# The text-and-image attention kernel: the first batch's value table copied inside the chip memory, the second batch's stored piece by piece

## The reference, cut to what matters

```python
q   = heads(x @ W_q)                                # x: 4 x 2048 x 640, 20 heads of 32
k_t, v_t = heads(text @ W_k), heads(text @ W_v)     # 73 text tokens per batch
probs_t  = softmax(q k_t^T * scale)
text_out = probs_t @ v_t
k_ip, v_ip = heads(ip @ W_k_ip), heads(ip @ W_v_ip) # 4 image tokens per batch
qsem  = l2norm(probs_t @ text);  ip_n = l2norm(ip)
fused = q k_ip^T * scale + 0.5 * (qsem . ip_n)
probs_ip = softmax(fused) * spatial_mask
out = (text_out + probs_ip @ v_ip) @ W_out + b_out + x
```

## Time and profile before

| | |
|---|---|
| three runs | 1017.63, 1020.25, 1022.09 us; median 1020.25 |
| the profiled execution | 1022.47 us, span 1020.6 us |
| TensorE clock granted, mean | 0.988 |
| prologue ends and main loop begins | 88.7 us into the span |
| step 16, the first with output products all through | 184.8 us |

### The profile page before, as it was taken

The page is one execution under the profiler, slowest core; times in us unless marked ns, Lnnn a source line. Parts: engine busy times, 40 slices in busy tenths (PEclk is TensorE's granted clock), DMA queues, the critical chain, the costliest instruction groups (busy, mean ns, idle before and its releaser), DMA issues.

```text
span 1020.6 us, 24929 instructions
## 1 busy us (share of the span) xinstructions
PE 969.2 (95%) x7684; PEld 803.6 (79%) x7684; DVE 816.6 (80%) x2409; ACT 695.6 (68%) x2332; POOL 655.2 (64%) x1906
## 2 busy tenths in 40 slices
PE   5987788999999999999999999999999999999988
PEld 5875666888878888888887888888878888888855
DVE  6685698888888887888888888878878888878872
ACT  3534887777776777767776777777667777777740
POOL 3224587776676667677766777676667767776761
PEclk9978999999999999999999999999999999999999
DMA  9936999989889998899899989998899989887973
GB/s 293 298 117 161 195 179 186 177 163 180 168 186 186 186 185 177 163 176 162 174 178 192 192 164 191 169 167 173 167 190 187 180 169 190 137 157 154 149 138 111
DMA packets 488147, 180.27 MB, mean 177 GB/s; under 512 B 449694, under 2 KB 467155, under 8 KB 488015
## 3 DMA queue, kind: packets, MB, share of 16 engines
q1 hardware_dynamic: 487983, 178.63, 86.3%
q10 hardware_dynamic: 32, 0.07, 0.0%
HBM read 42.34 MB, written 27.22 MB: 68 GB/s over the span
## 4 chain that ended last, share of the span: by engine, by line
PE 77%; DMA 5%; DVE 4%; ACT 2%; issue 2%; SPq 2%; POOL 1%; DVEq 0%; ACTq 0%; POOLq 0%
PE ps_O L1257 25%; PE ps_Q L1368 25%; PE ps_S L1278 12%; PE ps_U L1354 11%; DMA pts<-ph 4%; PE ps_M L1294 3%; ACT pr L1038 2%; DMA x_in<-in_x_dram 1%; SPq L951 1%; DVE pr L1199 0%; PE ps_U L1257 0%; DVE n L1211 0%; ACT ph L1050 0%; DVE bias L1160 0%; SPq L924 0%
## 5 line engine op out<-in xcount | busy, mean ns | idle before, releaser
L1038 ACT ACTIVATE pr<-ps_S,bias 128x73 f32<-128x73 f32 x1280 | 288.8, 339 | 101.3 <-DVE bias L1160 100.1
L1120 POOL TENSOR_TENSOR ph<-pr,ph 128x220 f16<-128x220 f32 (+1 forms) x640 | 274.0, 460 | 126.2 <-ACT ph L1050 126.2
L1368 PE MATMUL ps_Q<-xT,wq_hi 128*128 128x512 f32 x800 | 280.1, 415 | 5.2 <-DVE qT L1127 5.2
L1257 PE MATMUL ps_O<-wo_hi,aT 128*128 128x320 f16 x1220 | 279.2, 300 | 0.0
L1050 ACT ACTIVATE ph<-pr 128x292 f16<-128x292 f32 x640 | 241.2, 500 | 0.0
L1257 PE MATMUL ps_O<-wo_lo,aT 128*128 128x320 f16 x610 | 182.3, 299 | 0.0
L1354 PE MATMUL ps_U<-xm,pts 128*128 128x110 f16 (+1 forms) x2560 | 159.3, 212 | 14.9 <-DMA pts<-ph 13.5
L1368 PEld LDWEIGHTS ps_Q<-xT,wq_hi 128*128 128x128 f32 x800 | 146.2, 191 | 32.7 <-DVE qT L1127 6.5
L1354 PEld LDWEIGHTS ps_U<-xm,pts 128*128 128x128 f16 (+1 forms) x2560 | 144.4, 98 | 32.3 <-issue 11.8
L1278 PE MATMUL ps_S<-kbd,qT 128*128 128x308 f32 x960 | 163.0, 304 | 2.6 <-ACT pr L1038 2.1
L1278 PEld LDWEIGHTS ps_S<-kbd,qT 128*128 128x128 f32 x960 | 150.8, 188 | 18.6 <-issue 3.0
(11 more groups left out here) (228 smaller groups left out, 1338.9 us busy)
## 6 DMA issues: line engine op xcount, KB each, us to landing
out_dram<-x_in SPq DMA_DIRECT2D x64, 320.0 KB, 2.6
x_in<-in_x_dram SPq DMA_DIRECT2D x56, 320.0 KB, 3.2
pts<-ph SPq DMA_TRANSPOSE x320, 3.4
w_k<-in_L_xattn_W_k_dram SPq DMA_DIRECT2D x5, 512.0 KB, 8.8
w_ip<-in_L_xattn_W_k_ip_dram SPq DMA_DIRECT2D x1, 2560.0 KB, 11.0
w_v<-in_L_xattn_W_v_dram SPq DMA_DIRECT2D x5, 512.0 KB, 8.3
w_ip<-in_L_xattn_W_v_ip_dram SPq DMA_DIRECT2D x1, 2560.0 KB, 10.6
x_in<-in_x_dram SPq DMA_DIRECT2D x2, 1280.0 KB, 7.2
```

The costliest lines, as they stand in the source:

```text
L1038: last = nc.scalar.activation(pr[p % P_RING][:, j, h, :], sc[:, j, h, 0:T], ACT.Exp, bias=bias[p % 2][:, j, h:h + 1], scale=SCALE)
L1120: nc.gpsimd.tensor_tensor(lo, full[:, :, t0:t1], one[:, :, 0, t0:t1], ALU.subtract).then_inc(pl_ready, 1)
L1257: last = nc.tensor.matmul(bank[:, 0:HALF], stationary, moving, start=(k, a, b_) == O_MMS[0], stop=(k, a, b_) == O_MMS[-1])
L1368: last = nc.tensor.matmul(ps_Q[:], wq[a][:, c, k * P:(k + 1) * P], xT[(CC * i + c) % XT_RING][b_][:], start=(c, a, b_) == Q_MMS[0], stop=( ...
```

## The change

Batch 0's eight pieces go from `xb[0]` directly to their rows of `xm`; each counts on `xm_loaded[0]`. Its ten reads from `x_d` are gone, and the wait for the stores ahead of them. Batch 1's eight pieces are stored to `x_d` one a step in steps 2 to 9, at the head of SP's step. The two batches' halves of the buffer are moved so that batch 0's lies within `x_in[2]` and batch 1's within `x_in[3]`. SP awaits the direct copies before the first load of x tile 2 (step 1), and batch 1's stores before the first load of x tile 3 (step 11). PE awaits all eight copies before the first value product.

```diff
-        xb = [one[0:T, 0:4 * HEADS * XW].rearrange("t (b k h w) -> t b k h w", b=2, k=2, w=XW)
-              for one in (late0[:].bitcast(F16), late1)]
+        xb = [one[0:T].rearrange("t (b n) -> t b n", b=2)[:, :, 0:2 * HEADS * XW]
+              .rearrange("t b (k h w) -> t b k h w", k=2, w=XW) for one in (late0[:].bitcast(F16),)]
+        xb.append(late1[0:T, 0:4 * HEADS * XW].rearrange("t (b k h w) -> t b k h w", b=2, k=2, w=XW))
...
                 if p == FIRST:
                     for tile, row, part, t0, t1 in pieces:
-                        sp.dma_start(x_d[0:2, tile, row:row + t1 - t0].rearrange("b t h w -> t b h w"),
-                                     xb[0][t0:t1, :, part]).then_inc(x_d_stored, 16)
+                        sp.dma_start(xm[row:row + t1 - t0, tile], xb[0][t0:t1, 0, part]).then_inc(xm_loaded[0], 16)
+                if 0 <= p - 2 < len(pieces):
+                    tile, row, part, t0, t1 = pieces[p - 2]
+                    sp.dma_start(x_d[1, tile, row:row + t1 - t0], xb[0][t0:t1, 1, part]).then_inc(x_d_stored, 16)
...
-                        if p == max(2 * SLOTS * b + 2 * c - 6, FIRST):
-
-                            if b:
-                                sp.wait_ge(u_ready, 2 * (SLOTS * b + c) - 8)
-                            if c == 0 and b < 2:
-                                sp.wait_ge(x_d_stored, 16 * 8)
+                        if b and p == 2 * SLOTS * b + 2 * c - 6:
+
+                            sp.wait_ge(u_ready, 2 * (SLOTS * b + c) - 8)
                             for tile, n in enumerate(STACK):
                                 sp.dma_start(xm[0:n, tile, c * HG:(c + 1) * HG, :],
                                              x_d[b, tile, 0:n, c * HG:(c + 1) * HG, :]).then_inc(xm_loaded[c], 16)
...
                         if p == max(STEPS * j + LOAD_AT[q], FIRST):
+                            if j == 2 and q == 0:
+                                sp.wait_ge(xm_loaded[0], 16 * len(pieces))
+                            if j == 3 and q == 0:
+                                sp.wait_ge(x_d_stored, 16 * len(pieces))
...
-                        pe.wait_ge(xm_loaded[k0], 32 * (slot // SLOTS + 1))
+
+                        b = slot // SLOTS
+                        if b:
+                            pe.wait_ge(xm_loaded[k0], 32 * b + (0 if k0 else 16 * 8))
+                        elif k0 == 0:
+                            pe.wait_ge(xm_loaded[0], 16 * 8)
```

## The result

The changed kernel took 1024.03 us (median of seven runs, 1020.75 to 1026.07) against 1020.25 us before (seven runs, 1017.63 to 1022.52). The two medians differ by 3.8 us. The ratio estimated from all fourteen runs is 1.0031, 95% interval 1.0018 to 1.0045: slower by 0.31%, about 3.2 us, less than the 0.5% set as the bound.

A forecast was written before the change was run, and what follows sets the result against it. It took DVE and the DMA engines, with SP third, as near full in steps 2 to 9. Terms -0.1 + 0.2 + 0.3 + 0.5 + 0.9 + 0.4 = +2.2 us on 1020.25 gave 1022.4 us, range 1017.2 to 1026.6 us.

The forecast's parts named there:

- What bounds the kernel: Steps 2 to 9: DVE and DMA engines near full, SP third; PE full from step 16, so delay passes one to one.
- Part 1: Loop start: eight direct copies replace eight stores and eight reads; nothing on the path, -0.1 us.
- the sign that I had set against it: At the loop start: pair 0's transposes issued before 104.3 us would prove the start's forecast wrong.
- The cover: At the start: copies done by 93.0 to 101.0 us, far ahead of the first value product at 108.55 us.
- the bounds of the copies' own price: At the start, from 88.7 us: direct copies done between 93.0 us (4.3 us) and 101.0 us (12.3 us).
- Part 2: SP in steps 2 to 9: eight issues added, two reads removed; lateness 0 to 0.5 us a step, -0.2 in step 2.
- Part 3: DMA engines in steps 2 to 9: 941 KB added, 188.2 KB removed, 3.5 to 4.9 us more of all sixteen engines.
- What reaches the path: Steps 2 to 9: +0.2, +0.3, +0.5 in steps 2 to 4, 0 in 5 to 7, +0.9 in 8, +0.4 in 9.
- hidden: Rival, steps 2 to 9: DVE's work and SP's gaps absorb everything; total -0.3 to +0.8 us; chance 0.20.
- The start was the limit: Rival, steps 0 to 2: without reads and with SP free they come earlier, -0.5 to -3 us; chance 0.12.
- The full engines pass it all on: Rival, steps 2 to 9: each store delays every later transpose on full DMA engines, +3.5 to +6.5 us; chance 0.18.
- The Trainium skill's price: Steps 2 to 9: bytes over 436 GB/s, 2.2 us added and 0.4 us removed; total about +1 instead of +2.2 us.

The follow-up runs named there:

- e1: Changed kernel with batch 1's eight stores all at the main loop's start, behind the direct copies, none in steps 2 to 9; ratio 0.9997 to the kernel before.
- e2: Changed kernel with batch 0 again going through chip memory and its reads back, batch 1's stores still spread; ratio 1.0028 to the kernel before.
- e6: e1 plus eight tiny stores (64 bytes of each row) in steps 2 to 9; ratio 1.0010 to the kernel before.
- e4: The changed kernel unaltered, timed again and profiled a second time; ratio 1.0018 to the kernel before.
- e5: e1 with batch 3's eight stores also moved to the start, batch 2's left in steps 8 to 15; ratio 0.9996 to the kernel before.
- e10: e5 with batch 2's eight stores also at the start, issued by ACT; ratio 1.0017 to the kernel before.
- e12: e10 with batch 2's eight stores issued by POOL instead of ACT; ratio 1.0019 to the kernel before.
- e3: e1 with the sixteen stores of batches 3 and 2 also moved to the start, all issued by SP; ratio 1.0023 to the kernel before.
- e7: Changed kernel with the eight stores of steps 2 to 9 behind each step's transposes instead of ahead; ratio 1.0046 to the kernel before.
- e11: Changed kernel with the eight stores of steps 2 to 9 issued by ACT at its step's end instead of SP; ratio 1.0028 to the kernel before.

## Why the prediction was right, point by point

- *What bounds the kernel:* right as far as pair 36. The loss is made in the sixteen steps, and from pair 16 to 36 nothing is made up. That it goes into the time one to one is not shown: in the four kernels that spread the stores from SP the sixteen steps are 3.4 to 6.0 us longer than before, and the times 1.8 to 4.7 us. Its signs: pair 17's maximum, and with it step 16, came 2.3 us later (185.24 against 182.95 us), as forecast. The end of that one execution did not move with it (1020.0 against 1020.6 us), for the scatter told above; the runs together did.
- *Part 1, nothing on the path, -0.1 us:* right, though the sign that I had set against it came true: pair 0's transposes were issued at 103.15 us, before 104.3. The sign was badly chosen, since it counts from the span's start. Counted from pair 0's score maximum the transposes come after 4.6 us before and after, and in e1 and e2. What came earlier is pair 0 itself: 10.6 us after SP's first issue in place of 11.4. The granted clock, at half around the loop's start in every profile, rose 4.1 us after SP's first issue in the one after and 5.7 us after it before, and pair 0 follows that and not the direct copy: in e1, with the copy, it is 5.8 us and pair 0 comes after 11.5 us; in e2, without it, 4.1 us and 10.6 us. SP issued the eight copies in 5.56 us. The cover held, so the bounds of the copies' own price did not matter; no run measured that price.
- *Part 2, SP:* not refuted, and hardly tested. I had 1.7 us of lateness, of which part reached the path; e6, issues without bytes, has 1.5 us, but that is less than the 2.6 us between two profiles of one kernel, and 0.7 us of it is slower matmuls.
- *Part 3, the bytes:* the mechanism (stores ahead of the transposes make them land later) is seen, and my step list was not right. For step 2 I credited 0.9 us for the removed reads and came to +0.2 in all; the transposes landed 1.2 us later (5.6 against 4.4) and from pair 4 to pair 5 it was 7.3 us in place of 5.2. For step 6 I wrote 0 because DVE covered it: a store and an x quarter together stood ahead, landing went from 3.9 to 5.3 us, and PE waited 1.95 us. For step 4 I wrote +0.5: its transposes landed in 5.2 us in place of 4.5, and pair 4's product did not wait (in e4 it waited 1.72 us). For step 8 I wrote +0.9: they landed in 4.5 us in place of 3.9, and pair 8's product did not wait in either profile. For step 9 I wrote +0.4, and pair 9's product waited 0.90 us in place of 0.87. The share of the DMA engines from 113 to 154 us, which I expected at 1.05 to 1.15, was 1.00 before and after. The total was +2.2 us forecast, about 3.2 us measured by the first comparison and 1.8 us (0.0018 x 1021) by the second.
- *The step that failed* is "What reaches the path", read as a schedule. It put most of the loss at steps 4, 8 and 9 and nothing at step 6. Measured, the long waits are those of pairs 2 and 6 in both profiles of the changed kernel, with pairs 4, 9 and 11 in the second. Slack that one profiled execution shows in a step need not be there in the next.
- *Missing altogether:* the fall of TensorE's clock behind long waits, two or three times, up to 1.6 us each. The forecast had no term for it. By the account of PE's time the falls are 2.5 and 3.5 us in the two profiles, and the waiting, all that the forecast's +2.2 us was made of, 0.8 and 2.5 us. That the total came near is therefore in part luck: the waiting was put at the wrong steps, and in the first profile too high, and the term left out made up for it.
- *Rivals:* "hidden" fell with e2, whose interval is 1.2 to 4.5 us. "The start was the limit" fell with the 4.6 us from pair 0's maximum to its transposes, the same with and without the direct copy. "The full engines pass it all on" is the nearest and is not excluded. The time was under its +3.5 us in both comparisons (3.2 and 1.8 us), but the first one's interval reaches to 4.6 us, and the sixteen steps were 3.4 and 6.0 us longer. No run tells apart stores that pass on whole from stores that pass on in part with a fall of the clock on top.
- The Trainium skill's price (DMA: Bandwidth & Descriptors, Anatomy of one DMA) would have halved the bytes' part for a total of about +1 us. The section describes transfers issued by GpSimd, and these are issued by SP. The first comparison's interval, 1.8 to 4.6 us, excludes that; e4's, 0.4 to 3.3 us, does not.

## What to carry to other kernels

A transfer that nothing waits for is not free: ask when it is in the queues, and what is behind it there. Work moved out of a stretch in which SP waits and the DMA engines have room (a share of 0.71 from 88.7 to 101 us) into one in which both are nearly full, to save waiting that nobody did, lost here; keep it at the start, but stop before the first urgent transfer is due. Judge such a change by the stretch it touches, and take two profiles before believing in which step the loss is.

## What the runs showed of the hardware that was not expected

- With stores from a second queue, SP's own issues took longer: eight stores that took SP 4.3 us alone (e1, e5) took 5.9 us beside ACT's (e10) and 9.07 us in e12 with POOL's, and the eight direct copies 7.3 us in e10 against 5.5. In e12 SP's longest single issue, 2.64 us, began at 98.48 us, just as POOL's last one ended, while POOL's stores were still landing; so it is not only issuing at the same moment, and the runs do not tell more of the cause. SP alone, with all thirty-two in e3, needed at most 0.85 us for one. The Trainium skill (Trainium Kernel Development and Optimization, Key Constraints) says that issuing from several engines only saves the sequencer's issue time; in e12 not even that was saved: SP was done 19.6 us after its first issue with sixteen stores and eight copies, and after 19.7 us in e3 with all thirty-two on its own queue.
- The granted clock went to half for 3.4 us while PE was full again, shortly after PE had stood idle: most often 1.5 to 2.2 us for one landing, but in e6 1.72 us for DVE's `qT`, in e7's first fall 1.20 and 0.75 us for two landings, and in e2's second 0.97, 0.53 and 0.15 us. In e3, e11 and e12, where PE waited 3.25 to 3.83 us, it fell during the wait and stayed down for 6.8 to 6.9 us. Waits of 1.90 us (e4) and 1.88 us (e1) were followed by no fall.
